# Order of TensorE's high and low parts in the feed-forward products of a fused attention and FFN block

## The chip, the cores and the metric

The kernel runs on one core of a Trainium2 chip. The metric is the device time of one execution in microseconds. Three runs of the kernel before took 1507.88, 1507.97 and 1512.14 us; the median is 1507.97 us.

## The reference

```python
xn = layernorm(x)                                   # x: 16 x 512 x 256
x  = x + attention(xn) + ffn(xn)
# attention: linear attention, 16 heads, with elu(.) + 1, a projection, a layernorm with gamma and beta, + xn
# ffn, with ternary weights w and one scale s per output column:
tlin = lambda x, w, s: einsum('bsi,oi->bso', x, w) * s
h = silu(tlin(x, w1, s1)) * tlin(x, w2, s2)          # 256 -> 1024
h = gelu(tlin(h, h1, s3))                            # 1024 -> 1024
h = gelu(tlin(h, h2, s4))                            # 1024 -> 1024
return tlin(h, w3, s5)                               # 1024 -> 256
```

All inputs and outputs are 32-bit floats.

## The kernel before

**Tiles.** There are 16 tiles, one per batch row, of 512 tokens each. Tile 0 has an order of its own (`first_body`), tiles 1 to 14 run in a loop and tile 15 is the last, outside the loop (`body(t, more)`, with `more` false for the last). Each engine has its own order of work, written out by hand, and the engines wait for one another by semaphores.

**High and low parts.** A value is held in two parts. The high part is in `fp32r` and is made by ScalarE (L1349, L1357, L1362, L1367). The low part is the rest, in 16 bits, and is made by VectorE (L1724, L1731) after the high one. TensorE multiplies the high part with the weights in `fp32r` and the low part with the upper halves of the same weights in `bf16`; both add into the same PSUM bank. So each product is made of two types of matmul: a high one, with a weight load that the profile calls f32, and a low one, with a bf16 weight load.

**Gate stage.** `gate_group(t, o)` (L980 and on) runs eight times a tile, in the order of `GATE_ORDER`. A group writes two banks (gate and up), each from two chunks of the input; for each bank and chunk it does a high matmul and then a low one, with 512 columns each. There are three pairs of banks: the fourth group waits for the value that VectorE makes out of the first (L1715, after ScalarE's silu L1316), and so on. Between the groups stand parts of the attention (`kv_sums`, `apply_kv`).

**Hidden layers.** The two hidden layers are four steps of seven products each (a block scheme with seven products in place of eight); the weights of a product are sums of blocks, made once and kept in DRAM. The right side of a product is a block (`B11`, `B21`, `B22`) or a difference (`T1` to `T4`). The differences are made by GpSimd (L744 to L759), two of them by VectorE (L1749, L1756). `half_product(t, s, i, g)` does 4 high and 4 low matmuls of 256 columns for half of the inner dimension (`g`), and `product` does both halves: high, low, high, low. In steps 0 and 2 the order of TensorE is tied to the operands: it waits for each high and each low part (`hi_made`, `lo_made`); in steps 1 and 3 the operands are those of the step before, so no such wait is left. Every product waits for its bank to be free (`product_bank_read`) and for its weights (`ring_loaded`). The first three products of step 0 are done as first halves 1, 5, 6 and then second halves 1, 5, 6.

**After a product.** VectorE adds products together (L1762), ScalarE keeps the first one (L1374) and applies gelu (L1390), then the next operands are made. GpSimd issues the refills of the weight ring (L767), each after the end of a named product and in one queue with its differences: `refill(t, s, g)` stands between `t3`, `t4` and the like. In step 0, product 1 releases the first refill.

**Other work in the order of TensorE.** Within step 0 are the transposes of the attention's result (`to_rows`, L959), which wait for VectorE's stream transpose (L1700); within step 1 is the projection (`proj_step`, L886 to L888, all `fp32r`), within step 2 are the transposes of the next tile (L908). After step 3 come the next tile's q (`q_step`), the output groups (`out_group`, L1114) and its k and v (`kv_step`). An output group has four blocks of 4 high and 4 low matmuls with 256 columns.

Of the kernel before, what the change touches and what calls it, by code (L numbers as in the profile page):

```python
# [13 lines left out]
P = 128  # L14
B, N, D = 16, 512, 256
HID = 1024
# [110 lines left out]
GATE_PAIRS = 3  # L127

# [49 lines left out]
def block_kernel(nc, H, w_ffn, w_attn, vecs, rows, consts, out):  # L178
# [104 lines left out]
    def gate_bank(o, j):  # L283
        return ps[:, 2 * (GATE_ORDER.index(o) % GATE_PAIRS) + j, :]
# [282 lines left out]
    with block:  # L567
# [308 lines left out]
        def _(pe):  # L876
# [98 lines left out]
            def run(first, full):  # L975
# [3 lines left out]
                def gate_group(t, o):  # L979
# [10 lines left out]
                    for j, base in enumerate((W_GATE, W_UP)):  # L990
                        for k in range(DC):
                            wk = weights[:, base + k * HID + o * P:base + k * HID + (o + 1) * P]
                            for part in range(2):
                                if part == 1 and not full:
                                    r = mm(gate_bank(o, j), high_halves(wk),  # L995
                                           xnT_short[:, k, :], start=False, stop=k == DC - 1)
                                else:
                                    r = mm(gate_bank(o, j), wk, as_used(xnT[:, k, part, :]),  # L998
                                           start=k == 0 and part == 0, stop=k == DC - 1 and part == 1)
                    r.then_inc(gate_ready.sem, 1)  # L1000

                def half_product(t, s, i, g):
# [7 lines left out]
                    if g == 0:  # L1010
# [4 lines left out]
                    for part in range(2):  # L1015
                        if s % 2 == 0 and part == 0:
                            pe.wait_ge(*hi_made(t, group, block_of_b))
                        elif s % 2 == 0:
                            pe.wait_ge(*lo_made(t, group, block_of_b))
                        for m in range(2):  # L1020
                            for j in range(2):
                                begins = m == 0 and g == 0 and part == 0 and j == 0
                                ends = m == 1 and g == 1 and part == 1 and j == 1
                                if part == 1 and not full:
                                    r = mm(bank[:, m * HT:(m + 1) * HT],  # L1025
                                           high_halves(ring[:, place, 2 * g + j, m * P:(m + 1) * P]),
                                           short_lo_part(group, block_of_b)[:, j, :],
                                           start=False, stop=i in lasts and ends, skip_group_check=True)
                                else:
                                    r = mm(bank[:, m * HT:(m + 1) * HT],  # L1030
                                           ring_weights[:, place, 2 * g + j, m * P:(m + 1) * P],
                                           as_used(buf[:, j, slot[block_of_b], part, :]),
                                           start=i in firsts and begins, stop=i in lasts and ends,
                                           skip_group_check=True)
                    return r

                def product(t, s, i):
                    half_product(t, s, i, 0)
                    half_product(t, s, i, 1).then_inc(prod.sem, 1)

                def plain_product(s, n):
# [5 lines left out]
                    for g, group in enumerate(("G0", "G1") if s < 2 else ("H0", "H1")):  # L1047
                        parts = plain_operand(group, b)
                        for part in range(2):
# [4 lines left out]
                            for m in range(2):  # L1054
                                for j in range(2):
                                    if part == 0:
                                        wk = ring[:, PLAIN_PLACE[s][a], 2 * g + j, m * P:(m + 1) * P]
                                    else:
                                        wk = high_halves(ring[:, PLAIN_PLACE[s][a], 2 * g + j, m * P:(m + 1) * P])
                                    r = mm(bank[:, m * HT:(m + 1) * HT], wk, parts[part][:, j, :],  # L1060
                                           start=n < 4 and g == 0 and part == 0 and m == 0 and j == 0,
                                           stop=n >= 4 and g == 1 and part == 1 and m == 1 and j == 1,
# [3 lines left out]
                def plain_out_group(half):  # L1066
# [8 lines left out]
                    for at, (p, c) in enumerate(((0, c1), (0, c2), (1, c1), (1, c2))):  # L1075
                        for part in range(2):
                            pe.wait_ge(*(plain_hi, plain_lo)[part].after(0, f"O{p}{c}"))
                            for m in range(2):
                                k = 2 * p + m + (HK if c in ("C21", "C22") else 0)
                                wk = w_out[:, k * D:(k + 1) * D]  # L1080
                                for i in range(2):
                                    toks = slice(i * P, (i + 1) * P)
                                    r = mm(bank[:, i * D:(i + 1) * D],
                                           (hg[p][:, m, O_SLOT[c], 0, toks], hg_short[p][:, m, O_SLOT[c], 1, toks])[part],
                                           (wk, high_halves(wk))[part],
                                           start=at == 0 and part == 0 and m == 0 and i == 0,
# [1159 lines left out]
```

## Time and profile before

| | |
|---|---|
| profiled execution | 1507.92 us |
| its span | 1506.0 us |
| TensorE busy | 1486.2 us, 11020 matmuls |
| VectorE busy | 1167.9 us |
| ScalarE busy | 935.9 us |
| GpSimd busy | 467.3 us |
| TensorE's granted clock | 0.999 of full speed |
| DMA | 288.20 MB, 191 GB/s mean |

The profile is of one execution. Matmuls overlap in the array, and their ends are modelled, so "busy" is nearly 100% whatever their spacing; how fast TensorE goes is read from starts. In the timeline, instructions of one kind that follow one another are merged: the second column is the time from the first's start to the last's end, and "x4" is their number. "[0.80 <-DVE ...]" is idle time of the engine before the instruction, and what ended it. DVE is VectorE, ACT ScalarE, POOL GpSimd, PE TensorE.

### The profile page before, as it was taken

Reading aid. Unit: us, or ns where it says so; the run is one execution under the profiler, and the core shown is the slowest. Engines: PE = TensorE matmul, PEld = TensorE weight load, DVE = VectorE, ACT = ScalarE, POOL = GpSimd, SP = SyncE. Lnnn points to the kernel's source line nnn. Section 1 sums busy time; section 2 is a strip of 40 time slices with the busy share of each in tenths; the row PEclk is TensorE's granted clock in tenths of the full one; section 3 lists DMA queues with packets and bytes.
Section 4 is the critical chain, followed back from the end, with each engine's and each line's share of the span. In section 5 each row is a group of like instructions: output and inputs, shape, how many; then the busy total and the mean of one; then the engine's idle time right before and its main releaser. Section 6 shows DMA issues by size and latency. Waiting matters only on the chain.

```text
span 1506.0 us, 33314 instructions
## 1 busy us (share of the span) xinstructions
PE 1486.2 (99%) x11020; PEld 1228.6 (82%) x11020; DVE 1167.9 (78%) x2097; ACT 935.9 (62%) x1727; POOL 467.3 (31%) x554
## 2 busy tenths in 40 slices
PE   9999999999999999999999999999999999999998
PEld 5987978879698796987969878797887978879787
DVE  6857778787787877878778687786878878787787
ACT  4556657566575665756657566575765657656564
POOL 2213415134151331504325043240522405234151
PEclk9999999999999999999999999999999999999999
DMA  8796735637366372753727548184481844727454
GB/s 234 237 311 229 275 124 198 231 102 259 115 224 211 107 269 92 243 193 118 262 88 262 181 140 282 47 279 160 142 290 44 275 158 162 267 68 251 156 201 167
DMA packets 86419, 288.20 MB, mean 191 GB/s; under 512 B 7216, under 2 KB 46512, under 8 KB 63024
## 3 DMA queue, kind: packets, MB, share of 16 engines
q0 software_dynamic: 43296, 231.75, 45.1%
q1 hardware_dynamic: 42192, 54.29, 11.0%
q10 hardware_dynamic: 832, 1.18, 0.2%
q14 instruction: 80, 0.66, 0.1%
q8 instruction: 19, 0.31, 0.1%
HBM read 270.42 MB, written 25.17 MB: 196 GB/s over the span
## 4 chain that ended last, share of the span: by engine, by line
PE 90%; DVE 4%; issue 3%; DMA 1%; POOL 1%; ACT 0%; DVEq 0%; POOLq 0%; ACTq 0%
PE ps L1030 26%; PE ps L1025 25%; PE ps L1114 7%; PE ps L998 6%; PE ps L995 5%; PE ps L886 4%; PE ps L888 4%; PE ps L887 4%; PE ps L1060 4%; PE ps L949 2%; DVE zkv L1664 1%; PE ps L938 1%; PE ps L959 1%; PE ps L908 1%; DVE values_a L1715 1%
## 5 line engine op out<-in xcount | busy, mean ns | idle before, releaser
L1030 PE MATMUL ps<-operands_a,hidden_weights 128*128 128x256 f32 x2520 | 450.3, 301 | 0.4 <-DMA hidden_weights<-weight_blocks 0.3
L1025 PE MATMUL ps<-lo_a_in_bits,hidden_weights 128*128 128x256 f16 x2520 | 385.4, 275 | 0.1
L1030 PEld LDWEIGHTS ps<-operands_a,hidden_weights 128*128 128x128 f32 x2520 | 338.0, 189 | 7.6 <-issue 0.6
L1762 DVE TENSOR_TENSOR partial_sums<-partial_sums,ps 128x512 f32<-128x512 f32 x300 | 204.1, 685 | 123.8 <-PE ps L1025 74.9
L1724 DVE SCALAR_TENSOR_TENSOR lo_a_in_bits<-values_a,operands_a 128x512 f16<-128x512 f32 x315 | 236.0, 771 | 43.7 <-POOL values_a L759 20.6
L767 POOL DMA_DIRECT2D hidden_weights<-weight_blocks x236 | 135.2, 573 | 390.7 <-PE ps L1025 366.9
L998 PE MATMUL ps<-xnT,w_ffn 128*128 128x512 f32 x512 | 238.9, 567 | 10.2 <-DVE values_a L1715 10.2
L1025 PEld LDWEIGHTS ps<-lo_a_in_bits,hidden_weights 128*128 128x128 bf16 x2520 | 195.8, 98 | 45.2 <-DVE lo_a_in_bits L1724 2.9
L995 PE MATMUL ps<-xnT_lo_in_bits,w_ffn 128*128 128x512 f16 x512 | 200.2, 391 | 0.0
L1362 ACT ACTIVATE operands_a<-values_a 128x512 fp32r<-128x512 f32 x180 | 113.0, 628 | 71.4 <-POOL values_a L744 18.8
L744 POOL TENSOR_TENSOR values_a<-values_a 128x512 f32<-128x512 f32 x30 | 38.4, 1278 | 380.9 <-DVE values_a L1715 362.8
L995 PEld LDWEIGHTS ps<-xnT_lo_in_bits,w_ffn 128*128 128x128 bf16 x512 | 49.7, 97 | 126.3 <-issue 125.9
L1030 PE MATMUL ps<-operands_b,hidden_weights 128*128 128x256 f32 x840 | 150.8, 302 | 0.4 <-issue 0.4
L1390 ACT ACTIVATE values_out<-partial_sums,vectors 128x256 f32<-128x256 f32 x180 | 81.5, 501 | 90.7 <-DVE partial_sums L1762 90.7
L1316 ACT ACTIVATE gate_ring<-ps,vectors 128x512 f32<-128x512 f32 x128 | 85.8, 681 | 70.6 <-DVE values_a L1715 37.3
L1025 PE MATMUL ps<-lo_b_in_bits,hidden_weights 128*128 128x256 f16 x840 | 128.5, 275 | 0.5 <-DVE lo_b_in_bits L1724 0.5
L1715 DVE SCALAR_TENSOR_TENSOR values_a<-ps,vectors,gate_ring 128x512 f32<-128x512 f32 x128 | 93.9, 744 | 41.1 <-issue 30.8
L1030 PEld LDWEIGHTS ps<-operands_b,hidden_weights 128*128 128x128 f32 x840 | 112.5, 189 | 8.4 <-issue 6.0
L998 PEld LDWEIGHTS ps<-xnT,w_ffn 128*128 128x128 f32 x512 | 102.5, 200 | 14.7 <-DVE values_a L1715 14.0
L1731 DVE SCALAR_TENSOR_TENSOR lo_out_in_bits<-values_out,hidden_out 128x512 f16<-128x512 f32 x120 | 79.6, 686 | 36.4 <-ACT hidden_out L1367 36.4
L1408 ACT ACTIVATE exp_tmp<-zkv 128x256 f32<-128x256 f32 x64 | 26.6, 415 | 119.0 <-DVE q L1653 105.3
L1114 PE MATMUL ps<-w_out,hidden_out 128*128 128x256 f32 x464 | 81.1, 296 | 0.0
(161 smaller groups left out, 2762.2 us busy)
## 6 DMA issues: line engine op xcount, KB each, us to landing
hidden_weights<-weight_blocks POOLq DMA_DIRECT2D x180, 1024.0 KB, 5.3
hidden_weights<-weight_blocks POOLq DMA_DIRECT2D x60, 512.0 KB, 3.9
raw_weights<-weight_blocks SPq DMA_DIRECT2D x48, 304.0 KB, 2.8
hidden_weights<-in_w_ffn POOLq DMA_DIRECT2D x16, 512.0 KB, 7.8
weight_blocks<-weight_sums SPq DMA_DIRECT2D x16, 512.0 KB, 4.5
weight_blocks<-in_w_ffn SPq DMA_DIRECT2D x16, 512.0 KB, 10.6
out_dram<-acc SPq DMA_DIRECT2D x31, 256.0 KB, 2.2
x<-in_H SPq DMA_DIRECT2D x15, 512.0 KB, 5.6
```

Of the source, the lines that this page charges most:

```text
L767: pool.dma_start(of_ring(ring, g), part_weights((s + 1) % SETS, g)).then_inc(ring_loaded[g].sem, 16)
L995: r = mm(gate_bank(o, j), high_halves(wk), xnT_short[:, k, :], start=False, stop=k == DC - 1)
L998: r = mm(gate_bank(o, j), wk, as_used(xnT[:, k, part, :]), start=k == 0 and part == 0, stop=k == DC - 1 and part == 1)
L1025: r = mm(bank[:, m * HT:(m + 1) * HT], high_halves(ring[:, place, 2 * g + j, m * P:(m + 1) * P]), short_lo_part(group, block_of_b)[:, j, : ...
L1030: r = mm(bank[:, m * HT:(m + 1) * HT], ring_weights[:, place, 2 * g + j, m * P:(m + 1) * P], as_used(buf[:, j, slot[block_of_b], part, :]) ...
L1114: r = mm(bank[:, i * D:(i + 1) * D], hg_short[p][:, m, O_SLOT[c], 1, toks] if short else as_used(hg[p][:, m, O_SLOT[c], part, toks]), high ...
L1316: nc.scalar.activation(gate[:, n % 2, :], gate_bank(o, 0), ACT.Silu, scale=vec[:, V_GATE + o:V_GATE + o + 1]).then_inc(silu_made.sem, 1)
L1362: nc.scalar.activation(hi_part(group, block), value(group, block), ACT.Copy, scale=LIFT).then_inc(hi.sem, 1)
L1390: r = nc.scalar.activation(dst, src[:, m * HT:(m + 1) * HT], ACT.Gelu, scale=vec[:, col:col + 1])
L1715: v.scalar_tensor_tensor(out=ha_values[:, o % HK, first:first + 2, 1, :], in0=two(gate_bank(o, 1)), scalar=vec[:, V_UP + o:V_UP + o + 1], ...
L1724: v.scalar_tensor_tensor(out=part, in0=value(group, block), scalar=LIFT, in1=hi_part(group, block).bitcast(F32), op0=ALU.mult, op1=ALU.sub ...
L1762: v.tensor_tensor(scratch[:, dst, :], scratch[:, kept, :], product_bank(s, i), ALU.add).then_inc(add.sem, 1)
```

## The change

TensorE's instructions are the same ones; their order is another. A `quarter_product` (4 matmuls of one type) takes the place of `half_product`. `product` now does 8 high and then 8 low matmuls, or 8 low and then 8 high (`LO_FIRST`). In steps 1 and 3, where operands are not waited for, every other product is low first, so that the low parts of two products stand beside each other; so do the first products of steps 1, 2 and 3. The first three products of step 0 are high for three first halves, low for three first halves, low and high for the second half of product 1, high for 5 and 6, low for 5 and 6. A gate group does its four high and then its four low matmuls, low first in groups 1, 3 and 6 (counted from 0). The output groups go high, high, low, low, low, high, high, low over their blocks. Tile 0's plain products and its output groups are grouped in the same way. The last tile differs from the loop by a split product 2 in step 2 and by its last output group.

```diff
+LO_FIRST_GROUPS = (1, 3, 6)
+HI_FIRST, LO_FIRST = (0, 1), (1, 0)
...
-                    for j, base in enumerate((W_GATE, W_UP)):
-                        for k in range(DC):
-                            for part in range(2):
+                    parts = LO_FIRST if n in LO_FIRST_GROUPS else HI_FIRST
+                    for part in parts:
+                        for j, base in enumerate((W_GATE, W_UP)):
+                            for k in range(DC):
...
-                def half_product(t, s, i, g):
+                def quarter_product(t, s, i, g, part, begins=False, ends=False):
...
-                def product(t, s, i):
-                    half_product(t, s, i, 0)
-                    half_product(t, s, i, 1).then_inc(prod.sem, 1)
+                def product(t, s, i, parts=HI_FIRST):
+                    quarter_product(t, s, i, 0, parts[0], begins=True)
+                    quarter_product(t, s, i, 1, parts[0])
+                    quarter_product(t, s, i, 0, parts[1])
+                    quarter_product(t, s, i, 1, parts[1], ends=True).then_inc(prod.sem, 1)
...
+                    order = LO_FIRST if s % 2 == 1 and n % 2 == 0 else HI_FIRST     # plain products of tile 0
...
-                    order = ((0, c1), (0, c2), (1, c1), (1, c2)) if half == 0 else ((0, c1), (0, c2), (1, c2), (1, c1))
+                    steps = ((0, c1, 0), (0, c2, 0), (0, c2, 1), (0, c1, 1), (1, c2, 1), (1, c2, 0), (1, c1, 0), (1, c1, 1))
...
-                    half_product(t, 0, 1, 0)
-                    half_product(t, 0, 5, 0)
-                    half_product(t, 0, 6, 0)
-                    half_product(t, 0, 1, 1).then_inc(prod.sem, 1)
-                    half_product(t, 0, 5, 1).then_inc(prod.sem, 1)
-                    half_product(t, 0, 6, 1).then_inc(prod.sem, 1)
+                    quarter_product(t, 0, 1, 0, 0, begins=True)
+                    quarter_product(t, 0, 5, 0, 0, begins=True)
+                    quarter_product(t, 0, 6, 0, 0, begins=True)
+                    quarter_product(t, 0, 1, 0, 1)
+                    quarter_product(t, 0, 5, 0, 1)
+                    quarter_product(t, 0, 6, 0, 1)
+                    quarter_product(t, 0, 1, 1, 1)
+                    quarter_product(t, 0, 1, 1, 0, ends=True).then_inc(prod.sem, 1)
+                    quarter_product(t, 0, 5, 1, 0)
+                    quarter_product(t, 0, 6, 1, 0)
+                    quarter_product(t, 0, 5, 1, 1, ends=True).then_inc(prod.sem, 1)
+                    quarter_product(t, 0, 6, 1, 1, ends=True).then_inc(prod.sem, 1)
...
-                    product(t, 1, 1)
+                    product(t, 1, 1, LO_FIRST)
                     product(t, 1, 6)
                     proj_step(t, 0)
                     proj_step(t, 1)
                     product(t, 1, 2)
-                    product(t, 1, 5)
+                    product(t, 1, 5, LO_FIRST)
                     product(t, 1, 7)
-                    product(t, 1, 3)
+                    product(t, 1, 3, LO_FIRST)
                     product(t, 1, 4)
-                    product(t, 2, 1)
+                    product(t, 2, 1, LO_FIRST)
...
-                    product(t, 3, 1)
+                    product(t, 3, 1, LO_FIRST)
                     product(t, 3, 6)
-                    product(t, 3, 2)
+                    product(t, 3, 2, LO_FIRST)
                     product(t, 3, 5)
-                    product(t, 3, 7)
+                    product(t, 3, 7, LO_FIRST)
                     product(t, 3, 3)
-                    product(t, 3, 4)
+                    product(t, 3, 4, LO_FIRST)
```

## Rows read from the trace of the kernel before

**Rows 1.** The page, part 1: busy time of each engine over the span.
```profile
PE 1486.2 (99%) x11020; PEld 1228.6 (82%) x11020; DVE 1167.9 (78%) x2097; ACT 935.9 (62%) x1727; POOL 467.3 (31%) x554
```

**Rows 2.** Waits of TensorE, whole span: us in total, times, longest us.
```profile
PE ps L998 <- DVE values_a L1715: 10.2, 13, 1.0
...
PE ps L1025 <- DVE lo_b_in_bits L1724: 0.5, 1, 0.5
```

**Rows 3.** Timeline, gate stage of tile 5: start us, us, instruction, idle before.
```profile
495.23 1.41 DVE L1715 SCALAR_TENSOR_TENSOR values_a<-ps,vectors,gate_ring 128x512 f32<-128x512 f32 x2 [2.39 <-issue]
...
496.04 0.50 PE L998 MATMUL ps<-xnT,w_ffn 128*128 128x512 f32 x1 [0.80 <-DVE values_a L1715]
```

**Rows 4.** Timeline, step 3: a VectorE sum; two high runs, seven periods apart.
```profile
556.76 0.69 DVE L1762 TENSOR_TENSOR partial_sums<-partial_sums,ps 128x512 f32<-128x512 f32 x1 [3.28 <-ACT values_out L1390]
...
558.08 0.71 PE L1030 MATMUL ps<-operands_b,hidden_weights 128*128 128x256 f32 x4
...
564.56 0.72 PE L1030 MATMUL ps<-operands_a,hidden_weights 128*128 128x256 f32 x4
```

**Rows 5.** Timeline, projection of step 1: two high matmuls, 21 apart.
```profile
526.52 0.28 PE L888 MATMUL ps<-wproj_parts,attention_by_row 128*128 128x256 f32 x1
...
528.98 0.27 PE L888 MATMUL ps<-wproj_parts,attention_by_row 128*128 128x256 f32 x1
```

**Rows 6.** Timeline, two windows that cut one low run after three and four.
```profile
562.34 0.50 PE L1025 MATMUL ps<-lo_b_in_bits,hidden_weights 128*128 128x256 f16 x3
...
562.34 0.61 PE L1025 MATMUL ps<-lo_b_in_bits,hidden_weights 128*128 128x256 f16 x4
```

**Rows 7.** Timeline, gate stage: two high matmuls, seven pairs apart.
```profile
503.37 0.58 PE L998 MATMUL ps<-xnT,w_ffn 128*128 128x512 f32 x1
...
506.63 0.58 PE L998 MATMUL ps<-xnT,w_ffn 128*128 128x512 f32 x1
```

**Rows 8.** Timeline, q of the next tile: two high matmuls, nine apart.
```profile
566.03 0.39 PE L888 MATMUL ps<-xnT,wqkv_parts 128*128 128x512 f32 x1
...
568.13 0.40 PE L888 MATMUL ps<-xnT,wqkv_parts 128*128 128x512 f32 x1
```

**Rows 9.** Timeline, output group: two high runs, two periods apart.
```profile
569.21 0.72 PE L1114 MATMUL ps<-w_out,hidden_out 128*128 128x256 f32 x4
...
571.10 0.72 PE L1114 MATMUL ps<-w_out,hidden_out 128*128 128x256 f32 x4
```

**Rows 10.** Timeline, step 0: what the transposes and product 7 wait for.
```profile
511.40 0.63 ACT L1362 ACTIVATE operands_a<-values_a 128x512 fp32r<-128x512 f32 x1 [0.73 <-POOL values_a L749]
...
513.04 0.70 DVE L1700 STREAM_TRANSPOSE relu_tmp<-exp_tmp 128x512 f32<-128x512 f32 x1
...
513.80 1.22 PE L959 MATMUL ps<-constants,relu_tmp 128*128 128x128 f32 x8
...
515.40 2.30 DVE L1724 SCALAR_TENSOR_TENSOR lo_a_in_bits<-values_a,operands_a 128x512 f16<-128x512 f32 x3 [0.73 <-ACT operands_a L1362]
...
516.56 0.61 PE L1025 MATMUL ps<-lo_a_in_bits,hidden_weights 128*128 128x256 f16 x4
```

**Rows 11.** Timeline, steps 1 and 2: refill, difference, low parts, product 7.
```profile
539.10 0.53 POOL L767 DMA_DIRECT2D hidden_weights<-weight_blocks  x1 [1.47 <-PE ps L1025]
...
541.09 1.29 POOL L754 TENSOR_TENSOR values_a<-values_a 128x512 f32<-128x512 f32 x1
...
541.19 1.73 DVE L1724 SCALAR_TENSOR_TENSOR lo_a_in_bits<-values_a,operands_a 128x512 f16<-128x512 f32 x1
...
544.39 0.69 DVE L1724 SCALAR_TENSOR_TENSOR lo_a_in_bits<-values_a,operands_a 128x512 f16<-128x512 f32 x1 [1.47 <-POOL values_a L759]
...
545.82 0.73 PE L1030 MATMUL ps<-operands_b,hidden_weights 128*128 128x256 f32 x4
```

**Rows 12.** Timeline, a refill; the page, part 6: refills' time to landing.
```profile
537.06 0.57 POOL L767 DMA_DIRECT2D hidden_weights<-weight_blocks  x1
...
hidden_weights<-weight_blocks POOLq DMA_DIRECT2D x180, 1024.0 KB, 5.3
```

More of the change, by code:

```diff
@@ L1014, in half_product @@
                     buf, slot = operands(group)
[L1015 to L1034, printed above, removed]
@@ L1035, in half_product @@
-                    return r
-                def product(t, s, i):
-                    half_product(t, s, i, 0)
-                    half_product(t, s, i, 1).then_inc(prod.sem, 1)
+                    if s % 2 == 0 and part == 0:
+                        pe.wait_ge(*hi_made(t, group, block_of_b))
+                    elif s % 2 == 0:
+                        pe.wait_ge(*lo_made(t, group, block_of_b))
+                    for m in range(2):
+                        for j in range(2):
+                            wk = ring_weights[:, place, 2 * g + j, m * P:(m + 1) * P]
+                            if part == 1 and not full:
+                                wk, xk = high_halves(wk), short_lo_part(group, block_of_b)[:, j, :]
+                            else:
+                                xk = as_used(buf[:, j, slot[block_of_b], part, :])
+                            r = mm(bank[:, m * HT:(m + 1) * HT], wk, xk,
+                                   start=i in firsts and begins and m == 0 and j == 0,
+                                   stop=i in lasts and ends and m == 1 and j == 1, skip_group_check=True)
@@ L1046, in plain_product @@
                     pe.wait_ge(s_first[s][a], 16)
-                    for g, group in enumerate(("G0", "G1") if s < 2 else ("H0", "H1")):
-                        parts = plain_operand(group, b)
-                        for part in range(2):
+                    groups = ("G0", "G1") if s < 2 else ("H0", "H1")
+                    order = LO_FIRST if s % 2 == 1 and n % 2 == 0 else HI_FIRST
+                    for part in order:
+                        for g, group in enumerate(groups):
+                            parts = plain_operand(group, b)
                             if s % 2 == 0 and part == 0:
@@ L1060, in plain_product @@
                                     r = mm(bank[:, m * HT:(m + 1) * HT], wk, parts[part][:, j, :],
-                                           start=n < 4 and g == 0 and part == 0 and m == 0 and j == 0,
-                                           stop=n >= 4 and g == 1 and part == 1 and m == 1 and j == 1,
+                                           start=n < 4 and g == 0 and part == order[0] and m == 0 and j == 0,
+                                           stop=n >= 4 and g == 1 and part == order[1] and m == 1 and j == 1,
                                            skip_group_check=True)
```

107 lines of the change are left out of this document (53 added, 54 removed).

## The prediction

> **What bounds the kernel now.** I read the page first. TensorE is busy for 1486.2 of 1506.0 us, VectorE for 1167.9, GpSimd for 467.3 [rows 1], so a shorter TensorE order is the first thing that could shorten the kernel. Busy is not the same as waiting for nothing, so the waits come next. TensorE has one wait that repeats, 13 times and 10.2 us in all, for a gated value of VectorE; the others are single, and within the products the longest is 0.5 us [rows 2]. That wait stands in the gate stage: VectorE shows 2.39 us of "issue" after the last work of the tile before (that is where its loop turns over) and makes the first gated value at 495.23; TensorE goes on at 496.04 [rows 3]. Everywhere else TensorE's order is the clock, so I read starts of its matmuls, not durations, which are modelled and overlap.
>
> A half product (4 high, 4 low matmuls of 256 columns) takes (564.56 - 558.08) / 7 = 0.926 us [rows 4]. In a long run of high-part type, the projection's, one matmul takes (528.98 - 526.52) / 21 = 0.117 us [rows 5]. In a low run the step from the third to the fourth is 0.61 - 0.50 = 0.11 us [rows 6]; the rows are rounded to 0.01, so it is 0.105 to 0.115, and since 256 columns at the granted 2.4 GHz are 0.107, I take 0.109. Then 4 x 0.117 + 4 x 0.109 = 0.904, and 0.022 us of each half product is left over: the price of going from one type to the other and back (a "pair"). Its ends by the rounding are 0 and 0.038.
>
> The same for the gate: one high and one low of 512 columns take (506.63 - 503.37) / 7 = 0.466 us [rows 7]. A high one in a run takes (568.13 - 566.03) / 9 = 0.233 [rows 8]. No run of low ones with 512 columns exists in this trace; twice 0.109 is 0.218, from below it is 0.213 (512 columns at 2.4 GHz), from above 0.230. I take 0.218: 0.015 us a pair, ends 0.003 and 0.020. In the output groups a pair's period is (571.10 - 569.21) / 2 = 0.945 [rows 9]; low ones there were not seen alone, so I carry over 0.02.
>
> The Trainium skill (TensorE: Matmul & The Clock Gate, Back-to-back issue gap) gives columns / 2.4 GHz + 2.5 ns whatever the type, and in LDWEIGHTS says that the next weights are pulled ahead of running matmuls. By that rule, 109 ns each, a half product would be 0.87 us and a change of type would cost nothing. The low run agrees; the high run, 0.117, does not. If the remaining 0.022 were also something else than the change of type, this edit would bring nothing: a rival below.
>
> **The change, part by part.** No matmul, byte or wait is added or taken away; only the order differs, so I count low runs (each is one pair). Products of a loop tile: 28 with 2 low runs each, 56. After: the first three products 2 (were 6); the other four of step 0, 4, the last joined with the first of step 1; step 1 then 4, its last joined with step 2; step 2 then 6, its last joined with step 3; step 3 then 3. Sum 19, so 37 pairs go. Gate: 32 runs become 5 (27 go). Output: 8 become 4.
> Uncovered, a tile would gain 37 x 0.022 + 27 x 0.015 + 4 x 0.02 = 1.30 us. Not all of it is kept, because some waits are chains that TensorE's speed between their ends does not shorten:
>
> - Gate groups 1 to 3. TensorE waits at 496.04 for VectorE [rows 3], whose chain starts at TensorE's last matmul of the tile before. What these three groups save (11 pairs, 0.17) is eaten by the wait, which grows.
> - Gate groups 4 to 7: 16 runs become 3. 13 x 0.015 = 0.20, kept.
> - The last gate group and the first three products. VectorE's work from the seventh gate group's value on leads up to its stream transpose, which ends at 513.74, and TensorE's transposes of that result start at 513.80 [rows 10]: no room. 3 pairs of gate and 4 of product go before that point, 0.13 us, and TensorE must wait for them. Partly given back: product 1 now ends before its two partners' last quarters, 0.07 earlier against the block's start (3 pairs); GpSimd's refill and difference hang on it, behind them the low part that VectorE begins at 515.40, and on that TensorE's low matmuls of product 7 at 516.56: this start moves forward with product 1. I count 2 of the 5 product pairs up to there (with product 7) as kept.
> - The operands of the second half: high ones are wanted 0.47 us sooner after a product's start, low ones of the first half later. Hidden where the maker is well ahead. The tightest one that I find is the third product's high difference: ScalarE has it at 512.03 [rows 10], and it is used one half product and a bit, 1.0, before the transposes, at 512.8; after, it is used 4 high and 8 low matmuls before them, 1.36 with the pair, at 512.4. 0.4 is left, and 0.2 after what the gate group saves and the step from a result to its use. If it came late, the wait before the transposes would take the delay up, as VectorE is late there anyway.
> - Steps 0 and 1 up to product 3: 12 pairs, kept. Product 4 of step 1 waits for a sum at the end of a VectorE chain that starts with product 5; TensorE's part beside it (products 7 and 3) shrinks by 3 pairs, 0.07. That is the most that can go, nothing the least; I take 0.04 off.
> - Step 2's first four products. When step 1 ends, GpSimd issues a refill (539.10), then a small chain, then a difference at 541.09; VectorE's low part at 541.19 takes 1.73 us; another difference follows; VectorE makes the next low part from 544.39, the sum after it, and TensorE starts product 7 at 545.82 [rows 11]. This chain of 7.3 us does not depend on TensorE between its ends, and TensorE has no room there. 5 pairs lost, 1 (product 4 of step 1) kept.
> - From there to the end of step 3: 14 pairs, kept. The sum of step 3 at 556.76 ends at 557.45, 0.63 before its bank is written at 558.08 [rows 4]; it starts from a TensorE product itself, so it moves along.
> - Output: 4 pairs, 0.08, kept; the high and low parts that it reads are made from step 2's and 3's sums while the next tile's first projections run. If they were late, no more than the 0.08 would go.
>
> Weights cost nothing: the tightest refill of step 2, products 7 and 2, is issued at 537.06 and such a transfer of 1 MB lands in 5.3 us, at 542.4 [rows 12]; its first use, product 2, is one product before 545.82 [rows 11], at about 543.9. 0.2 us less cover leaves over one. Without that cover TensorE would wait the rest of a landing.
>
> Sum for a loop tile: pairs 2 + 12 + 1 + 14 = 29, 29 x 0.022 = 0.64; gate 0.20; output 0.08; minus 0.04: 0.88. Fourteen tiles: 12.3 us. Tile 0, in plain products: 64 low runs become 24, 40 x 0.022 = 0.88, output 0.08; of the gate I count nothing, as the first product there meets a wait: 0.96. The last tile has VectorE's additional checks and its own waits [rows 2]; half a loop tile's and a bit, 0.5. Total 13.8 us. The profiled execution took 1507.92 us (span 1506.0, 1.9 around it), the median of the runs is 1507.97: the same. 1507.92 - 13.8 = 1494.1.
>
> **Rivals.**
> (a) Everything is kept, 1.30 a tile: if the chains move with TensorE because their starts do. 14 x 1.30 + 0.96 + 0.42 + 1.2 = 20.8, 1487.1. For it: TensorE sets nearly all starts. Against: rows 10 and 11 have room of 0.1 us at most. Chance 0.12.
> (b) The chains of steps 0 and 1 eat all up to product 4 as well, since VectorE is busy for 78% of the span [rows 1]; kept are 14 pairs and the output, 0.39 a tile and 1 in the ends: 6.5, 1501.4. Chance 0.15.
> (c) The 0.022 is no price of a change of type, or long low runs are slower: no gain, 1507.9. For it: the value rests on a rounding. Against: the high run of the projection is 24 long and keeps 0.117. Chance 0.05.
> (d) Slower. VectorE's low part took 1.73 us at 541.19 where GpSimd's difference had started 0.10 before and ended at 542.38 [rows 11]; the like of it alone takes 0.69, so a meeting costs 1.04 us. The edit moves GpSimd (which starts at a product's end) against VectorE by 0.05 to 0.15. If two more low parts in TensorE's tight places begin just inside a difference, 2 x 1.04 - 0.88 = +1.2 a tile, +17 us: 1525; it decides from the second on, one is about no change (1510). Against: most differences wait for a VectorE result, so they start behind it. Chance 0.05.
> The Trainium skill (SBUF — State Buffer, Who interferes with whom) says that a VectorE instruction with two SBUF inputs and a GpSimd one that reads SBUF block each other, by order of issue. The 1.73 us agrees; by that rule (d) needs a start inside the other's run, no more.
>
> **How the numbers follow.** The forecast has 0.63, with its own range 1489 to 1499 (pair price 0.030 to 0.014). For 8 in 10 I add the greater part of (a) and of (b): 1486.5 to 1502. A measurement of this kernel can tell about 0.3%, 4.5 us, from no change. Faster: 0.63 + 0.12 + most of (b) = 0.89; same: (c) and rests, 0.06; slower 0.05.
>
> **What would show it.** In the profile after: a product that stands alone takes 1.83 us (two half products took 1.85), and two whose low parts meet take 3.64 (3.70). A tile from the first gate matmul to the next takes 91.9 us. The wait for the gated value grows from 0.80 to about 0.95; short new waits of 0.1 to 0.2 stand before the transposes of step 0 and at product 7 of step 2. Wrong would be: a product that still takes 1.85 (c); low parts of 1.7 us in new places (d); TensorE waits over 0.5 a tile beyond the one known (b).

## The result

The changed kernel took 1492.4 us (median of 4 runs, 1491.61 to 1492.85) beside 1507.93 us for the kernel before (4 runs, 1506.96 to 1512.14). Its time is 0.9892 of the other, 95% interval 0.9878 to 0.9906: 15.5 us faster. The forecast was 1494.1, from 1486.5 to 1502. The profiled execution took 1491.61 us with a span of 1489.8, 16.2 under the span before.

Busy times of the changed kernel, part 1 of the profile's page, beside [rows 1], and its waits of TensorE (us in total, times, longest), beside [rows 2]:

```profile
PE 1468.5 (99%) x11020; PEld 1268.2 (85%) x11020; DVE 1167.3 (78%) x2097; ACT 935.6 (63%) x1727; POOL 466.0 (31%) x554
```

```profile
PE ps L1000 <- DVE values_a L1723: 12.1, 13, 1.1
...
PE ps L1029 <- DVE partial_sums L1770: 0.8, 1, 0.8
PE ps L1062 <- DVE lo_a_in_bits L1746: 0.5, 1, 0.5
```

The same 11020 matmuls, the other engines unchanged to 0.3%. The one repeated wait grew from 10.2 to 12.1 us: something was gained in front of it and lost in it.

I measure by tile periods, from a tile's first gate matmul to the next tile's. First the start of tile 2 and of tile 15 (the last) in the timeline of the kernel before, then the same two of the changed one (the x3 is four matmuls cut by the window):

```profile
210.22 0.40 PE L998 MATMUL ps<-xnT,w_ffn 128*128 128x512 f32 x1
...
1416.14 0.40 PE L998 MATMUL ps<-xnT,w_ffn 128*128 128x512 f32 x1
```

```profile
207.78 1.10 PE L1002 MATMUL ps<-xnT,w_ffn 128*128 128x512 f32 x4
...
1401.38 0.86 PE L1002 MATMUL ps<-xnT,w_ffn 128*128 128x512 f32 x3
```

(1416.14 - 210.22) / 13 = 92.76 us, (1401.38 - 207.78) / 13 = 91.82: 0.95 a tile (forecast 0.88). Tile 0 gained 1.06, the last tile 1.45, the 14 loop tiles 13.3; together 15.8. The other 0.37 of the 16.2 is the prologue, ahead of the first gate matmul: 19.60 us before, 19.23 after, and 19.25 to 20.28 in the profiles of the experiments, which left it alone. So it is scatter and no part of the gain. A period averages 13 tiles whose lengths scatter by about 0.1 us, so I trust it to about 0.03 us; the one kernel that was run twice (below) gave 90.80 and 90.78. Times of separate sets of runs repeat less well; where a difference is under 2 us, I go by periods.

Where in a tile it came from (median of tiles 2 to 14, TensorE's starts, us):

| stretch of a tile | before | after | both | products alone | gates and outputs alone |
|---|---|---|---|---|---|
| gate stage, to the first product | 19.51 | 19.06 | -0.46 | -0.04 | -0.41 |
| first three products of step 0 | 5.67 | 5.72 | +0.05 | -0.01 | +0.06 |
| transposes to the projection | 12.27 | 12.08 | -0.20 | -0.15 | -0.06 |
| projection to the end of product 7 of step 2 | 21.57 | 21.44 | -0.13 | -0.13 | +0.01 |
| next transposes to the end of q | 20.59 | 20.37 | -0.22 | -0.21 | 0.00 |
| outputs, kv | 13.13 | 13.09 | -0.03 | 0.00 | -0.03 |

(The last two columns are the first two experiments. Medians do not add up exactly; the differences are of unrounded values. The ends of the stretches stand where the type before them is the same in all kernels, because a high matmul behind a low one is recorded about 0.08 us early: the two steps around such a start are 0.03 and 0.20 us, where two high ones take 0.23 together.)

Step 3 of the changed kernel; high runs of 16 and low runs of 16, in fours as the operands' names change:

```profile
553.37 0.60 PE L1029 MATMUL ps<-lo_a_in_bits,hidden_weights 128*128 128x256 f16 x4
...
554.25 0.60 PE L1029 MATMUL ps<-lo_a_in_bits,hidden_weights 128*128 128x256 f16 x4
554.60 0.72 PE L1029 MATMUL ps<-operands_b,hidden_weights 128*128 128x256 f32 x4
555.16 0.64 PE L1029 MATMUL ps<-operands_a,hidden_weights 128*128 128x256 f32 x4
...
556.10 0.64 PE L1029 MATMUL ps<-operands_a,hidden_weights 128*128 128x256 f32 x4
...
557.03 0.60 PE L1029 MATMUL ps<-lo_a_in_bits,hidden_weights 128*128 128x256 f16 x4
...
557.90 0.60 PE L1029 MATMUL ps<-lo_a_in_bits,hidden_weights 128*128 128x256 f16 x4
558.26 0.72 PE L1029 MATMUL ps<-operands_b,hidden_weights 128*128 128x256 f32 x4
```

Two products whose parts meet: 558.26 - 554.60 = 3.66 us (forecast 3.64; before 3.70, four times the 0.926 of [rows 4]). In the runs a high matmul takes (556.10 - 555.16) / 8 = 0.1175 and a low one (554.25 - 553.37) / 8 = 0.110 or (557.90 - 557.03) / 8 = 0.109. The rows are rounded to 0.01; the unrounded starts of tiles 2 to 14 give 0.1185 in long high runs and 0.109 in low ones, but 0.121 for the first step of each low run.

A product that stands alone, and the transposes and product 7, in step 0 of the changed kernel, beside [rows 10]:

```profile
507.10 1.05 PE L1029 MATMUL ps<-lo_a_in_bits,hidden_weights 128*128 128x256 f16 x8
508.11 1.23 PE L962 MATMUL ps<-constants,relu_tmp 128*128 128x128 f32 x8
509.09 1.28 PE L1029 MATMUL ps<-operands_a,hidden_weights 128*128 128x256 f32 x8
510.22 1.18 PE L1029 MATMUL ps<-lo_a_in_bits,hidden_weights 128*128 128x256 f16 x8
511.15 1.19 PE L1029 MATMUL ps<-operands_a,hidden_weights 128*128 128x256 f32 x8
512.18 1.05 PE L1029 MATMUL ps<-lo_a_in_bits,hidden_weights 128*128 128x256 f16 x8
512.98 1.19 PE L1029 MATMUL ps<-operands_a,hidden_weights 128*128 128x256 f32 x8
```

512.98 - 511.15 = 1.83 us, as forecast. Eight low matmuls from 507.10 would end their starts at 507.98; the transposes start at 508.11: the new short wait, 0.1 longer than before.

The gate stage, beside [rows 3], timeline of VectorE and TensorE:

```profile
489.89 1.41 DVE L1723 SCALAR_TENSOR_TENSOR values_a<-ps,vectors,gate_ring 128x512 f32<-128x512 f32 x2 [2.36 <-issue]
490.70 1.04 PE L1000 MATMUL ps<-xnT_lo_in_bits,w_ffn 128*128 128x512 f16 x4 [0.96 <-DVE values_a L1723]
491.39 0.81 PE L1002 MATMUL ps<-xnT,w_ffn 128*128 128x512 f32 x2
```

The wait now ends in front of a low run, at 7.4 us from the start of the tile as before, and shows 0.96 where it showed 0.80.

The chain behind step 1, beside [rows 11], timeline of GpSimd, VectorE and TensorE:

```profile
533.14 0.53 POOL L770 DMA_DIRECT2D hidden_weights<-weight_blocks  x1 [1.44 <-PE ps L1029]
...
535.20 1.69 DVE L1732 SCALAR_TENSOR_TENSOR lo_a_in_bits<-values_a,operands_a 128x512 f16<-128x512 f32 x1
...
539.77 0.73 PE L1029 MATMUL ps<-operands_b,hidden_weights 128*128 128x256 f32 x4
```

6.63 us from refill to product 7; before it was 545.82 - 539.10 = 6.72. VectorE's low part under GpSimd's difference takes 1.69 us as before (1.73), and no other low part of this tile shows such a length (two take 1.1 us, in both kernels).

### The profile page after: what moved, and what is told of

The parts are those of the page before. It is cut to its first block, busy times and chain, and to the rows that moved or that the text cites. A ratio compares the mean times of both kernels' runs of the same rounds, so it can differ in the third digit from the quotient of the medians.

```text
span 1489.8 us, 33314 instructions
## 1 busy us (share of the span) xinstructions
PE 1468.5 (99%) x11020; PEld 1268.2 (85%) x11020; DVE 1167.3 (78%) x2097; ACT 935.6 (63%) x1727; POOL 466.0 (31%) x554
## 4 chain that ended last, share of the span: by engine, by line
PE 92%; DVE 4%; issue 3%; DVEq 0%; ACT 0%; POOL 0%; POOLq 0%; ACTq 0%
PE ps L1029 52%; PE ps L1114 7%; PE ps L1002 5%; PE ps L1000 5%; PE ps L889 4%; PE ps L891 4%; PE ps L890 4%; PE ps L1062 4%; PE ps L952 2%; DVE zkv L1672 1%; PE ps L962 1%; PE ps L941 1%; PE ps L911 1%; DVE values_a L1723 1%; DVE partial_sums L1831 1%
## 5 line engine op out<-in xcount | busy, mean ns | idle before, releaser
L1029 PE MATMUL ps<-operands_a,hidden_weights 128*128 128x256 f32 x2520 | 368.3, 285 | 0.1
L1029 PE MATMUL ps<-lo_a_in_bits,hidden_weights 128*128 128x256 f16 x2520 | 337.2, 273 | 0.0
L1029 PEld LDWEIGHTS ps<-operands_a,hidden_weights 128*128 128x128 f32 x2520 | 323.8, 189 | 1.8 <-DVE partial_sums L1770 0.5
L1029 PEld LDWEIGHTS ps<-lo_a_in_bits,hidden_weights 128*128 128x128 bf16 x2520 | 232.7, 98 | 34.9 <-DVE lo_a_in_bits L1732 3.3
L1002 PE MATMUL ps<-xnT,w_ffn 128*128 128x512 f32 x512 | 150.5, 421 | 0.0
L1029 PE MATMUL ps<-operands_b,hidden_weights 128*128 128x256 f32 x840 | 146.8, 296 | 0.8 <-DVE partial_sums L1770 0.8
L1000 PE MATMUL ps<-xnT_lo_in_bits,w_ffn 128*128 128x512 f16 x512 | 126.8, 381 | 12.1 <-DVE values_a L1723 12.1
L1002 PEld LDWEIGHTS ps<-xnT,w_ffn 128*128 128x128 f32 x512 | 93.0, 189 | 21.2
L1000 PEld LDWEIGHTS ps<-xnT_lo_in_bits,w_ffn 128*128 128x128 bf16 x512 | 42.7, 98 | 78.9 <-issue 22.0
L1029 PEld LDWEIGHTS ps<-lo_b_in_bits,hidden_weights 128*128 128x128 bf16 x840 | 71.3, 98 | 12.4 <-DVE lo_b_in_bits L1732 0.2
```

Source lines behind the costliest of these rows:

```text
L1000: r = mm(gate_bank(o, j), high_halves(wk), xnT_short[:, k, :], start=begins, stop=ends)
L1002: r = mm(gate_bank(o, j), wk, as_used(xnT[:, k, part, :]), start=begins, stop=ends)
L1029: r = mm(bank[:, m * HT:(m + 1) * HT], wk, xk, start=i in firsts and begins and m == 0 and j == 0, stop=i in lasts and ends and m == 1 and ...
```

## The experiments

**1 and 2: the change in two parts.** The change with `gate_group`, `out_group`, `plain_out_group` and `last_out_group` as before, and the opposite:

```
e1_products:    gate_group: for j: for k: for part     (new: for part: for j: for k)
                outputs:    c1 hi, c1 lo, c2 hi, c2 lo, ...
e2_gates_outs:  product = half_product 0, half_product 1, each hi then lo
```

> The change with its products in the new order, and its gate and output groups back in the order of the kernel before. By the prediction's terms the products keep 29 pairs of type changes a tile at 0.022 us, 0.64 us a tile, 9 us over 14 tiles, with about 1 us more in the first and the last tile: 10 us of the 15.5 us gained, so about 1497.9 us, and the steps behind the gates each keep the length that they have in the changed kernel. Rival 1 (the gate and output groups carry more than their count, because they stand ahead of every chain): 1501 or more. Rival 2 (gates give nothing, their pairs go into the wait for VectorE's first gated value): 1493.5, only the output groups' 1 us missing.

> The kernel before with the new order in the gate and output groups alone. By the prediction's terms the gates keep 0.20 us a tile and the outputs 0.08, 4 us over 14 tiles and about 0.5 at the ends: about 1503.5 us, with the wait for the first gated value grown from 0.80 to 0.95 us a tile. Rival 1 (gates keep every pair): 0.40 + 0.08 a tile, 1500.5. Rival 2 (gates lose all to the wait): 1506.5. If the parts add, this gain and that of the products alone sum to the 15.5 us of both.

Measured: 1502.93 us for the products (0.9954 of the kernel before, 0.9937 to 0.9971), period 92.23, 0.54 less; 1501.26 for gates and outputs (0.9951, 0.9936 to 0.9966), period 92.33, 0.44 less. The parts add: 0.97 against 0.95. But they are sized otherwise than forecast: products 0.54 where 0.60 was counted (0.64 - 0.04), gates and outputs 0.44 where 0.28 was. Both results lie nearer to rival 1 of their expectations (1501 or more; 1500.5) than to the number that I expected: the gates give more than I had counted. But the reason named in rival 1 of experiment 2, that every gate pair is kept, is wrong (experiment 5 shows that ten are lost); experiment 8 finds part of the true one.

The 1502.93 needs a word, since 14 loop tiles at 0.54 and 0.7 in tile 0 would bring the first one from 1508.2 to about 1500; two of its five runs are there (1499.56 and 1500.44). In its profiled execution (1503.29 us) the last tile took 3.4 us longer than in the kernel before. Timeline of VectorE and TensorE there, then windows of it (us, busy times, TensorE's clock, DMA):

```profile
1455.19 0.79 DVE L1868 SCALAR_TENSOR_TENSOR low_bits<-raw_weights,low_bits 128x608 uint32<-128x608 uint32 x1 [4.08 <-DMA raw_weights<-in_w_ffn]
...
1456.64 1.49 PE L1029 MATMUL ps<-lo_a_in_bits,hidden_weights 128*128 128x256 f16 x8 [3.33 <-DVE partial_sums L1772]
```

```profile
1450.00:1465.00 15.00, 11.67 (x89) 10.73 (x88) 9.98 (x23) 5.26 (x12) 4.64 (x7) 0.89 0.74 256
...
1456.00:1457.00 1.00, 0.36 (x4) 0.33 (x5) 1.00 (x2) 0.00 (x0) 0.00 (x0) 1.00 0.24 79
...
1458.00:1459.00 1.00, 1.00 (x7) 1.00 (x6) 0.91 (x2) 0.00 (x0) 0.06 (x1) 0.50 0.14 54
```

VectorE stands 4.08 us for a transfer of weights that it only checks, a sum stands behind the check, and TensorE waits 3.33 us for the sum. The granted clock is still 1.00 (2.4 GHz) during the wait; it falls to 0.50 (1.2 GHz) at 1457.09, 0.45 us after TensorE goes on, and is back at 1.00 at 1460.51, which makes the 0.89 of the whole stretch. Of the other profiles only that of experiment 6 shows such a wait (3.53 us). That the two other runs near 1503 had it too is likely and not shown. So the sum of the parts is read from periods.

**3 and 4: does the change of type have a price?** Steps 1 and 3 of the kernel before with more changes of type, and with none:

```
e3_runs_of_2:  for s odd:  (hi, m 0) (lo, m 0) (hi, m 1) (lo, m 1)    was (hi, m 0) (hi, m 1) (lo, m 0) (lo, m 1)
e4_one_type:   for s odd, part 1:  weights in full, operand part 0    was high_halves(weights), the short low part
```

> The kernel before, with steps 1 and 3 of tiles 1 to 15 in runs half as long: 2 high, 2 low, 2 high, 2 low in each half of a product in place of 4 and 4; same operands, same waits. 28 pairs of type changes more a tile. If a pair costs 0.022 us: 0.62 us a tile, 9.2 us over 15 tiles, about 1517 us, and a half product 0.97 us where it was 0.927. Rival (the change of type costs nothing, the gain came from other orders and banks): 1507.9 us and 0.927 us.

> The kernel before, with the low matmuls of steps 1 and 3 of tiles 1 to 15 replaced by a second pass over the high operands (the low part of these products is left out, so the output is not the reference's): 8 high matmuls in each half product and no change of type. If a pair of changes costs 0.022 us: 8 x 0.117 = 0.936 us a half product against 0.927, 28 halves, 0.25 us a tile, +4 us: 1512. Rival (no price of a change; something of each half product, its first matmul or its waits, costs the 0.02 us): 4 x 0.008 us more for the type of the low matmuls and nothing back, 0.032 x 28 x 15 = +13.4 us: 1521.

Measured for runs of 2: 1515.33 us (1.0051 of the kernel before, 1.0035 to 1.0068), period 93.26, 0.50 more: 0.50 / 28 = 0.018 us a pair, where 0.022 was said and 0 by the rival. For one type: 1514.3 us (1.0047, 1.0030 to 1.0063), between the two sizes, 6.1 us more where the one said 4 and the other 13.4. Timeline of TensorE in step 3, runs of 2:

```profile
566.38 0.48 PE L1032 MATMUL ps<-operands_b,hidden_weights 128*128 128x256 f32 x2
566.70 0.39 PE L1027 MATMUL ps<-lo_b_in_bits,hidden_weights 128*128 128x256 f16 x2
566.85 0.48 PE L1032 MATMUL ps<-operands_a,hidden_weights 128*128 128x256 f32 x2
...
567.80 0.48 PE L886 MATMUL ps<-xnT,wqkv_parts 128*128 128x512 f32 x1
```

Three periods of 2 + 2 take 1.42 us: 0.947 for eight, beside 0.926 in runs of 4. And one type only:

```profile
560.32 0.63 PE L1025 MATMUL ps<-operands_b,hidden_weights 128*128 128x256 f32 x4
...
566.95 0.63 PE L1025 MATMUL ps<-operands_a,hidden_weights 128*128 128x256 f32 x4
```

56 high matmuls in 6.63 us, 0.118 each, not the 0.117 of the projection [rows 5]. So eight take 0.947, and with 0.109 for a low one inside a run (above) a pair of changes in runs of 4 costs 0.926 - 4 x 0.118 - 4 x 0.109 = 0.018; from the periods, 4 x 0.009 - 0.46 / 28 = 0.020. The price exists and is 0.018 to 0.020 by these three ways of reading it (0.016 at the least, with 0.1185 for a high one). 0.022 was too much because a high matmul of a product was taken 0.001 too cheap; the 0.109 of a low one was right.

**5 and 6: are the pairs lost where a chain sets the end?**

```
e5_gates_1to3_old:  if n < 3 and t > 0:  steps = [(part, j, k) for j for k for part]
e6_step2_old:       products 1, 5, 6, 2 of step 2:  quarters (g0 hi) (g0 lo) (g1 hi) (g1 lo)
```

> The changed kernel with gate groups 1 to 3 of tiles 1 to 15 (all that TensorE does of the gates before it waits for VectorE's first gated value) back in the alternating order: 11 pairs of changes more a tile. The prediction's step: they only end earlier in front of a wait whose end VectorE sets, so 1492.4 us, the wait back from 1.05 to about 0.9 us in the median tile, its end 7.4 us behind the start of the tile as now. Rival (they were kept in part): 11 x 0.015 us = 0.17 a tile, 1495.0 us.

> The changed kernel with the first four products of step 2 of tiles 1 to 15 back in the order of the kernel before, 5 pairs of changes more a tile. The prediction's step: the chain behind step 1 (a refill, GpSimd's difference, two low parts) eats them, so 1492.4 us and a wait at product 7 of step 2 gone to 0.05. Rival, what the two traces say: the chain starts with TensorE's own reads and moves with them, the pairs were kept, and 5 x 0.018 x 15 = 1.4 us come back: 1493.8 us, the wait at product 7 as before near 0.15 us.

Measured, gate groups: 1493.73 us (0.9909, 0.9894 to 0.9924), period 91.84 against 91.82. The edit brings ten pairs a tile back (the last low matmul of the third group runs on into the fourth group's, behind the wait), and they are worth 0.03, not 0.17; the forecast's step holds. The profiled executions lie 2.1 us apart, but 1.05 of that is in the prologue (20.28 us beside 19.23), where nothing was edited. The wait shrinks by what they would have given, here its row beside the 12.1 of the changed kernel:

```profile
PE ps L1005 <- DVE values_a L1728: 10.1, 13, 1.0
```

Step 2: 1492.92 us (0.9901, 0.9886 to 0.9916), period 91.88. Of the 0.06 more, the wait of the gate stage, which is not touched, has 0.09; from the projection to the end of product 7 the tile takes as long as in the changed kernel (21.45 against 21.44), and the wait at product 7 falls by 0.08 by TensorE's starts. The five pairs are lost in the chain, as predicted. My rival, read from the two traces beforehand, was wrong: the wait there looked the same before and after (0.15 and 0.17) only because the chain in front of it had become 0.09 shorter (6.72 to 6.63, above); that the order of step 1 did this is argued, not shown.

**8: what stands first behind a wait.**

```
LO_FIRST_GROUPS = (1, 6)     was (1, 3, 6)
```

> The changed kernel with gate group 4, the one behind the wait, high part first. It adds 1 pair of changes a tile, 0.02 us. Theory: a first matmul behind a wait shows its weight load and the next one's, which for a high matmul (189 ns a load) cost 0.1 us more than for a low one (97 ns), and this is why group 4 gained 0.16 us a tile where its pairs are worth 0.06: 0.12 us a tile, 1494.2 us. Rival (the first matmul's type does not matter behind a wait): 1492.7 us.

Measured: 1494.42 us (0.9918, 0.9904 to 0.9931), period 91.92, 0.10 more. Timeline of TensorE, group 4 behind the wait and the first matmul after it:

```profile
491.75 1.20 PE L1002 MATMUL ps<-xnT,w_ffn 128*128 128x512 f32 x4 [0.90 <-DVE values_a L1723]
492.79 1.04 PE L1000 MATMUL ps<-xnT_lo_in_bits,w_ffn 128*128 128x512 f16 x4
493.67 0.61 PE L941 MATMUL ps<-zkv 128*128 128x129 f32 x4
```

1.92 us for the group; in the changed kernel 492.50 - 490.70 = 1.80. The whole gate stage, whose two ends have the same types around them in both, takes 19.18 against 19.06. One pair explains 0.02 of the 0.12. The rest agrees with the loads of weights, 189 ns for a high and 98 for a low one; groups of part 5 of the profile's page for the changed kernel (busy, mean ns):

```profile
L1002 PEld LDWEIGHTS ps<-xnT,w_ffn 128*128 128x128 f32 x512 | 93.0, 189 | 21.2
L1000 PEld LDWEIGHTS ps<-xnT_lo_in_bits,w_ffn 128*128 128x128 bf16 x512 | 42.7, 98 | 78.9 <-issue 22.0
```

That it is the load and nothing else of the first matmul is argued, not shown.

**7: the wait itself.** VectorE's "issue" of 2.36 us stands where its loop turns. Its instructions keep their order; only the place of the turn moves:

```
 prologue; tile 0; head(1)
 for t in 2 .. 14:  tail(t - 1); head(t)      was  for t in 1 .. 14: head(t); tail(t)
 tail(14); head(15); tail(15)
 # tail begins at add_u(t, 3), where VectorE stood 3.24 us for ScalarE
```

> The changed kernel with VectorE's loop turned elsewhere: its instructions stand in the same order, but the loop closes ahead of the first sum of step 3, where VectorE sat idle 3.24 us, and not ahead of the first gated value, where it stood 2.36 us with nothing to wait for while TensorE waited 1.05 us for that value. If the stall is the turn of the loop, it moves into the idle time: the first gated value comes 2.3 us earlier, TensorE's wait goes, and the small waits of step 0 behind it (0.16 and 0.09 us) go with it: 1.05 to 1.3 us a tile, 14 tiles, 1474 to 1478 us. Rival (the stall belongs to the first instruction of a tile, wherever the loop closes): 1492.4 us. Second rival (ScalarE's first gate activation, which ends 0.6 us behind the turn's start, is the next to be late): half of it, 1485 us.

> The changed kernel with only the loop turned elsewhere once more, on the same chip as the three others, since differences of 2 us are read between them: 1480 us again, a tile period of 90.70 us.

Measured: 1480.07 us (0.9817, 0.9803 to 0.9830), and again 1480.09 (0.9812, 0.9799 to 0.9826), periods 90.80 and 90.78: 12.3 us under the changed kernel and 27 to 28 under the kernel before. TensorE's wait in the gate stage is gone. (By its starts it was 1.27 us between two low matmuls less 0.22 for one, 1.05, in the changed kernel, and 0.94 before; the profile shows 0.89 and 0.77. The expectations go by starts.) That is 2 us short of the 1478 that I expected at most. The gate stage, VectorE and TensorE (tile 5 starts at 481.26):

```profile
485.43 1.40 DVE L1736 SCALAR_TENSOR_TENSOR values_a<-ps,vectors,gate_ring 128x512 f32<-128x512 f32 x2
...
485.67 1.18 PE L1015 MATMUL ps<-xnT,w_ffn 128*128 128x512 f32 x4
486.69 1.90 PE L1013 MATMUL ps<-xnT_lo_in_bits,w_ffn 128*128 128x512 f16 x8
```

The first gated value starts 4.17 us behind the start of the tile (was 6.62), and low matmuls of groups 3 and 4 run through without a gap. The idle time before the sum of step 3 is no longer than before, so the turn is hidden whole:

```profile
547.51 0.69 DVE L1783 TENSOR_TENSOR partial_sums<-partial_sums,ps 128x512 f32<-128x512 f32 x1 [3.25 <-ACT values_out L1411]
```

The small waits of step 0 did not go with it: from the last low matmul to the transposes TensorE takes 0.25 us here as in the changed kernel, and 0.13 in the kernel before. So they do not hang on VectorE's backlog from the turn. That part of the expectation was wrong.

**9 and 10: what the change is worth without that wait.**

```
e9_turn_in_before:    the kernel before + the turn moved
e10_turn_gates_old:   experiment 7 + gate_group as before
```

> The kernel before with VectorE's loop turned ahead of the first sum of step 3, nothing else. It takes away the wait of 0.94 us in the median tile under which the pairs of gate groups 1 to 3 were lost. In the changed kernel the same move was worth 1.09 us a tile and 12.3 us in all; here the wait is 0.11 us shorter: 1496.5 us, a tile period of 91.77 us. If that holds, the whole change is worth 1.06 us a tile with the wait gone against 0.95 with it, and the 0.11 us between them are the pairs of gate groups 1 to 3. Rival (the wait of the kernel before ends with something else): less than 9 us gained.

> The changed kernel with the loop turned elsewhere and all gate groups of the order before. With no wait in the gates every one of their 27 pairs counts: 27 x 0.015 = 0.41 us a tile, period 91.11 us, 1486 us. Rival 1 (the last gate group's 4 pairs go into the wait before step 0's transposes, as the prediction had it): 0.35, 1485. Rival 2 (the kernel's gain in the gates came from low matmuls behind the wait, not from pairs): 0.1 or less, 1481.5.

Measured: 1495.71 us (0.9917, 0.9903 to 0.9930), period 91.80, and 1487.22 us (0.9870, 0.9846 to 0.9894), period 91.27. So without the wait the whole change is worth 91.80 - 90.79 = 1.01 a tile, and 15.6 us. That is 0.06 over the 0.95 with the wait, where I expected 0.11, and the 0.06 are no more than twice the scatter of a period. The gate stage goes from 18.48 to 18.00 us for 27 pairs: 0.018 a pair. With the wait it gained 0.46, nearly as much: the ten pairs in front of the wait come in without it, and the 0.10 for the low run behind the wait (8) goes. The gates as a whole are worth 0.48 a tile and 7 us, somewhat more than the 0.41 expected.

**11: filling the last chain's wait.** In experiment 7's kernel:

```
 product(t, 2, 2); transposes(t + 1, 0); transposes(t + 1, 1); product(t, 2, 7)
                            # was: product 2, product 7, transposes, transposes
```

> The changed kernel with the loop turned elsewhere and the next tile's transposes (1.02 us of TensorE, their input long made) ahead of product 7 of step 2 and not behind it, in tiles 1 to 14. They fill the wait of 0.17 us at product 7 for the chain behind step 1: 0.17 x 14 = 2.4 us, 1477.7 us. Rival (product 7's later start, 0.85 us, delays the sum that step 3's operands wait for): 1480 or more, with a new wait at the start of step 3.

Measured: 1489.98 us (0.9877, 0.9862 to 0.9892), 9.9 us slower than experiment 7, period 91.53. The wait at product 7 went, but behind product 7 there is a new one in each of the 14 tiles, 0.86 us (the other two of the 16 in the row stand in step 3 of tile 5 and in the last tile); waits of TensorE, and its row in the timeline of one tile:

```profile
PE ps L1042 <- DVE partial_sums L1783: 13.4, 16, 0.9
```

```profile
541.63 0.60 PE L1042 MATMUL ps<-lo_a_in_bits,hidden_weights 128*128 128x256 f16 x4
543.09 0.73 PE L1042 MATMUL ps<-operands_b,hidden_weights 128*128 128x256 f32 x4 [0.86 <-DVE partial_sums L1783]
```

Products 7 and 4 of step 2 share a bank (`product_bank`), and 4 must wait until VectorE has added 7 from it (`product_bank_read`); the transposes between them had covered that read. The rival had the sign and put the wait in the wrong place (start of step 3).

## Why the prediction was right, and where it was not

- *A pair of type changes has a price, and 68 of them go a tile.* Right (3 and 4): every tile goes from 96 low runs to 28. The size was off: 0.018 to 0.020 us for 256 columns, not 0.022; 0.018 for 512, not 0.015, as a low matmul of 512 columns takes 0.216 and was taken for 0.218. The trace of before held no long run of a product's own matmuls, and with rows rounded to 0.01 us a difference of four small numbers was the weakest number of the sum. So rival (c) is out.
- *Products, 29 pairs kept, 0.60 a tile.* Measured 0.54 (1), of which 0.04 stands in the gate stage, where nothing was changed. The count holds with 0.018: 29 x 0.018 = 0.52.
- *Gate groups 1 to 3 go into the wait.* Right: 0.03 of 0.17 kept (5). They are 10 pairs and not 11, and groups 4 to 7 are 14 and not 13; the 27 is right. Of the 0.11 us between the waits of the two kernels, 0.06 appear as gain once the wait is away (9).
- *Gate groups 4 to 7 are worth 0.20.* This is the term that was mis-sized: the gates gave 0.41 up to the projection (2: -0.41 + 0.06 - 0.06). 14 pairs at 0.018 are 0.25; 0.08 comes from the low run that now stands first behind the wait (8), which the prediction did not see as it read only the pair; and the last group's 3 pairs, 0.05, which it gave up, were lost before the transposes (+0.06) and came back between them and the projection (-0.06).
- *A new wait before the transposes.* Right, 0.1. *Given back in part:* more than the 2 pairs that were counted; from the transposes to the projection products alone gain 0.15, and gates alone give back all that they had lost.
- *Step 2's first four products lose their 5 pairs.* Right (6), though not by the row that I had named as its sign; that wait went from 0.15 to 0.17 only. The chain's 7.3 us in the prediction do not come out of [rows 11]: from the refill to product 7 they give 6.72.
- *Outputs, 0.08 a tile.* 0.03. That is 0.008 us for each of the 4 pairs where a product's cost more than twice that; no run was made for them alone, and why is open.
- *Tile 0, 0.96; last tile, 0.5.* 1.06 and 1.45. In the last tile of the kernel before TensorE waited three times, 0.33, 0.44 and 0.47 us; the changed one's profile shows one wait there, 0.78. That is 0.46 of the 1.45. One execution each is not enough to say that the order took them away.
- *Nothing slows down (rival d).* Right: 1.69 us for the low part under a difference, and no second such place.

The sum, 0.88 against 0.95 a tile, was nearer than its terms: products and outputs 0.11 too high, gates 0.2 too low. That these nearly cancel is luck; what the experiments bear out is the list of what is kept and what two waits swallow.

## What to carry to other kernels

Where a busy engine's order is the clock, give each edit a price per tile and then ask which chain between two of its waits would swallow it; here two chains swallowed 15 of 68 pairs (10 and 5), and undoing them one by one showed it. Price the thing in long runs before trusting a difference of rounded rows, and look at what stands first behind a wait. The largest gain was not in the order at all: the turn of another engine's loop cost 2.36 us in front of a wait, and closing the loop where that engine stands idle anyway gave 12.3 us. And before work is moved into a wait, see what that work covers where it stands now (11).

## What the hardware showed that I had not expected

- The turn of VectorE's loop costs 2.36 us where it stands before dependent work, and nothing in 3.25 us of idle time.
- A group of eight 512-column matmuls behind a wait takes 1.80 us with its low half first and 1.92 with its high half first.
- A high matmul of 256 columns takes 0.118 us in runs of products of 16 as of 56, and a low one 0.109 inside a run; going from high to low and back costs 0.018 to 0.020 us besides. In the gate stage a high load of weights takes 0.189 us and a low one 0.098.
- TensorE's granted clock stayed at 1.00 through a wait of 3.33 us, fell to 0.50 (1.2 GHz) 0.45 us after it went on, and stayed there for 3.4 us (profile of experiment 1). In that of experiment 6 it fell 1.1 us before the end of a wait of 3.53 us and stayed at 0.50 for 6.8 us.
